# Cross attention as one pipeline over 64 units of head and batch with token-major queries; the mixer's group ends in another order, and TensorE's groups without a jump

## What is computed

```
# mixer, heads h in 8 groups of 16
hBC = silu(causal_conv(x @ Wx.T))            # hs, B, C
Y   = ((C B^T) * L_h * causal) (hs * dt) + hs * D_h   # L_h: decays of head h
g   = Y * silu(x @ Wgate.T)
out = (g * rsqrt(mean(g*g over a group)) * norm_w) @ out_proj_w.T

# cross attention, 32 query heads, 8 key heads, dimension 128
kv = concat([context, latents], axis=1)      # 128 + 128 tokens
q, k, v = rms_norm(x @ Wq) * qw, rms_norm(kv @ Wk) * kw, kv @ Wv
probs = softmax(q k^T / sqrt(128))           # 4 query heads share a key head
out = concat_heads(probs v) @ Wo
```

## Time and profile before

| | us |
|---|---|
| runs before, median of 3 | 2788.09 (2783.61 to 2791.59) |
| the profiled execution | 2793.43 |
| its span, first to last instruction | 2791.7 |
| TensorE busy in it | 2566.3 (92%) |
| VectorE, ScalarE, GpSimd busy | 1808.0, 1081.7, 1052.3 |
| mean granted TensorE clock | 0.970 |

### The profile page before, as it was taken

One profiled execution on the slowest core, in us unless ns is written; L12 is line 12 of the kernel. 1 busy time (PEld: TensorE's weight loads), 2 busy tenths in 40 slices (PEclk: granted clock), 3 DMA queues, 4 the chain that ended last, 5 costly groups with the idle time before them and its releaser, 6 DMA issues. The chain is left out here.

```text
span 2791.7 us, 40903 instructions
## 1 busy us (share of the span) xinstructions
PE 2566.3 (92%) x14344; PEld 2096.7 (75%) x14344; DVE 1808.0 (65%) x2448; ACT 1081.7 (39%) x2197; POOL 1052.3 (38%) x838
## 2 busy tenths in 40 slices
PE   7876799999999999999999999899999999999958
PEld 5444687777877778777777887788888888888846
DVE  4865696785967858769588696455463554645553
ACT  2322343333433333334334333454454444544421
POOL 3001464554655555456454565312222122222210
PEclk9988899999999999999999999999999999999989
DMA  4000331330312313213132131100100001000010
GB/s 144 1 1 16 117 118 46 110 109 32 136 53 84 114 39 120 83 66 111 44 122 98 49 110 46 31 20 23 30 17 24 19 23 30 19 23 19 12 53 31
DMA packets 61515, 163.36 MB, mean 59 GB/s; under 512 B 8336, under 2 KB 8976, under 8 KB 52944
## 3 DMA queue, kind: packets, MB, share of 16 engines
q1 hardware_dynamic: 59232, 158.14, 16.5%
q10 hardware_dynamic: 2160, 3.43, 0.4%
HBM read 158.92 MB, written 2.62 MB: 58 GB/s over the span
## 5 line engine op out<-in xcount | busy, mean ns | idle before, releaser
L196 PE MATMUL pair<-XH,d_w_hi 128*128 128x512 f32 x1160 | 479.6, 413 | 58.5 <-DVE d_gated L1394 21.2
L197 PE MATMUL pair<-XL,d_w_hi 128*128 128x512 f32 x1160 | 466.3, 402 | 0.0
L198 PE MATMUL pair<-XH,d_w_lo 128*128 128x512 f32 x1160 | 465.1, 401 | 0.0
L1371 DVE TENSOR_TENSOR_SCAN d_decay<-d_decay,m_delta 128x1024 f32<-128x1024 f32 x128 | 366.2, 2866 | 47.7 <-DMA d_decay<-token_decays 47.7
L1270 POOL TENSOR_TENSOR d_decay<-d_decay,d_cb 128x1024 f32<-128x1024 f32 x128 | 309.1, 2415 | 135.5 <-DVE d_decay L1371 125.5
L196 PEld LDWEIGHTS pair<-XH,d_w_hi 128*128 128x128 f32 x1160 | 222.6, 192 | 122.6 <-issue 41.5
L1251 POOL TENSOR_TENSOR d_w_lo<-d_w,d_w_hi 128x512 fp32r<-128x512 f32 x144 | 192.3, 1336 | 314.7 <-ACT d_w_hi L1131 314.7
L198 PEld LDWEIGHTS pair<-XH,d_w_lo 128*128 128x128 f32 x1160 | 222.6, 192 | 54.7
L197 PEld LDWEIGHTS pair<-XL,d_w_hi 128*128 128x128 f32 x1160 | 222.8, 192 | 48.0
L1356 DVE SCALAR_TENSOR_TENSOR d_hs<-pair,d_conv,d_hs 128x1016 f32<-128x1016 f32 (+2 forms) x192 | 242.9, 1265 | 20.7 <-ACT d_hs L1156 16.2
L1275 POOL TENSOR_TENSOR d_gated_lo<-d_gated,d_gated_hi 128x512 fp32r<-128x512 f32 x128 | 165.2, 1294 | 210.3 <-ACT d_gated_hi L1175 210.3
(11 more groups left out here) (275 smaller groups left out, 6083.7 us busy)
## 6 DMA issues: line engine op xcount, KB each, us to landing
d_decay<-token_decays SPq DMA_DIRECT2D x64, 1024.0 KB, 4.9
d_w<-in_L_w_groups SPq DMA_DIRECT2D x144, 256.0 KB, 2.7
e_w<-in_L_w_heads SPq DMA_DIRECT2D x80, 256.0 KB, 2.6
d_wo<-in_L_wo_groups SPq DMA_DIRECT2D x64, 256.0 KB, 4.9
X<-in_x SPq DMA_DIRECT2D x8, 256.0 KB, 10.7
b_ctx<-in_ctx SPq DMA_DIRECT2D x8, 256.0 KB, 11.8
e_ctx<-in_ctx_t SPq DMA_DIRECT2D x4, 512.0 KB, 5.1
out<-X SPq DMA_DIRECT2D x8, 256.0 KB, 2.0
```

What stands on the lines that cost most here:

```text
L196: pe.matmul(out, wh, xh, start=first, stop=False)
L197: pe.matmul(out, wh, xl, start=False, stop=False)
L198: return pe.matmul(out, wl, xh, start=False, stop=last)
L1371: v.tensor_tensor_scan(r, r, m["DELTA"][:], 0.0, ALU.mult, ALU.add).then_inc(q["decay"], 1)
```

## The change

**Attention** becomes one sequence of U = 64 units n = kh * 8 + b, written out on every engine, with no loop. Queries of a unit are projected token-major for the four query heads of the key head at once (`project_q(n)`, 12 matmuls of 512, the tokens stationary), copied by VectorE (`q_copy`), squared and summed by ScalarE in four instructions (`q_sq`), and turned by TensorE in four transposes (`turn_q`); `q_ssq` is gone. A unit's power of the sum of squares is one GpSimd instruction over four columns, 64 in all in place of 32 over eight. Keys have bank 0 alone, queries bank 1. Weights of queries and of the output have two sets of buffers, K and V one; raw weights have four slots in place of two, and are converted in the order of `ITEMS`, two per unit in the first five units of a head. X is turned in two banks at the end.

**Mixer.** TensorE's seven groups are unrolled (the other engines keep the loop). At a group's end the projection of the next group's item 0 moves ahead of the last gate, item 1 goes to the TURN pair, `out` writes banks 6 and 7, `cb` moves behind batch 0 of `out`, and the sum of squares of batch 0 into the middle of batch 1. VectorE and ScalarE follow. The load of the next group's first decays is issued at j = 7. In the last group six items of attention weights are converted, GpSimd's part between the two halves of `gated_lo`, and the context in pieces of one batch; GpSimd instead of VectorE makes its low halves.

Core of the diff:

```diff
...
+K_ITEM, V_ITEM, O_ITEM, NI = 4, 5, 6, 10
+FIRST_ITEMS, ITEMS = (4, 5, 0, 1, 2, 3, 6, 7, 8, 9), (0, 1, 2, 6, 3, 7, 8, 9, 4, 5)
+EARLY = 6
+def weights_in(n):
+    kh, b = n // NB + 1, n % NB
+    if kh == HK:
+        return ()
+    return [NI * kh + x for x in ((0, 1), (2, 3), (4, 5), (6, 7), (8, 9), (), (), ())[b]]
...
+    def w_hi(self, act, m):
+        kh, i = self.item(m)
+        act.wait_ge(self.w_in[m % 4], 16 * (m // 4 + 1))
+        if i < K_ITEM and kh > 1:
+            act.wait_ge(self.q["q_proj"], NB * (kh - 1))
+        elif K_ITEM <= i < O_ITEM and kh:
+            act.wait_ge(self.q["kv_proj"], NB * kh)
+        elif i >= O_ITEM and kh > 1:
+            act.wait_ge(self.q["out_ready"], NB * (kh - 1))
+        act.activation(self.halves(m)[0], self.WR[:, m % 4, :], ACT.Copy).then_inc(self.q["w_hi"], 1)
+    def w_lo(self, pool, m):
+        hi, lo = self.halves(m)
+        pool.wait_ge(self.q["w_hi"], m + 1)
+        pool.tensor_tensor(lo, self.WR[:, m % 4, :], hi.bitcast(F32), ALU.subtract).then_inc(self.q["w_split"], 1)
...
         def proj_pair(i):
-            return GATES if i == 1 or i in GATE_OF else IN
+            return TURN if i == 1 else GATES if i in GATE_OF else IN
+        def out_bank(b):
+            return c.bank[6 + b % 2]
...
+                def decays(g, j):
+                    if j == BC_SLOT:
+                        sp.wait_ge(q["cb_ready"], START + g + 1)
+                    else:
+                        sp.wait_ge(q["y_ready"], START + g * JT + j - RSLOT + 1)
+                    sp.dma_start(R[:, j % RSLOT, :, :].rearrange("p h t -> p (h t)"),
+                                 rows[bass.ds(g, 1), j, :].broadcast_to([P, 2 * T])
+                                 ).then_inc(rows_in[j % RSLOT], 16)
                 def group(g, last_group=False):
                     for j in range(JT):
-                        if j == BC_SLOT:
-                            sp.wait_ge(q["cb_ready"], START + g + 1)
-                        else:
...
+                        if j:
+                            decays(g, j)
+                        if j == JT - 1 and not last_group:
+                            decays(g + 1, 0)
...
                     elif i == 1:
-                        pe.wait_ge(q["gated"], START + g * JT)
+                        pe.wait_ge(q["xdt"], START + g * JT)
                     elif i in GATE_OF and GATE_OF[i] == 0:
-                        pe.wait_ge(q["tap"], START + 3 * (g * NU + units(1)[-1] + 1))
+                        pe.wait_ge(q["acc"], START + g * NB)
...
+                    pe.wait_ge(q["gated"], START + (g + 1) * JT)
+                    def ssq(b):
...
+                    for b in range(NB):
+                        pe.wait_ge(q["acc"], START + g * NB + b - 1)
+                        for j in range(JT):
+                            if j % 4 == 0:
+                                pe.wait_ge(q["g_lo"], START + 2 * (g * NB + b) + j // 4 + 1)
+                            x = (j // 4) % 2
+                            last = three_pass(pe, out_bank(b)[:, :], GH[:, x, j % 4, :], GL[:, x, j % 4, :],
+                                              WOH[:, j, :], WOL[:, j, :], j == 0, j == JT - 1)
+                            if j % 4 == 3:
+                                last.then_inc(q["out_ready"], 1)
+                            if b == 1 and j == 3:
+                                ssq(0)
+                        if b == 0 and not last_group:
+                            cb(g + 1)
+                        if b:
+                            ssq(b)
...
                         project(g, gate_item(j))
                         scan(g, j)
                     turn_hs(g, JT - 1)
+                    if not last_group:
+                        project(g + 1, 0)
                     project(g, gate_item(JT - 1))
                     scan(g, JT - 1)
                     if not last_group:
-                        project(g + 1, 0)
                         project(g + 1, 1)
                         project(g + 1, 2)
-                        cb(g + 1)
                     out(g, last_group)
...
-                with pe.Fori(0, GM - 1) as g:
+                for g in range(GM - 1):
...
-                    if not last_group:
-                        silu(g + 1, 2)
                     for b in range(1, NB):
...
+                        if last_group:
+                            if b == 1:
                                 act.wait_ge(q["gate_ready"], START + GM * JT)
-                            act.wait_ge(e.w_in[i % 2], 16 * (i // 2 + 1))
-                            act.activation(e.weight(e.WH, i), e.WR[:, i % 2, :], ACT.Copy).then_inc(e.q["w_hi"], 1)
+                            if b <= EARLY:
+                                e.w_hi(act, b - 1)
...
+                            gated_lo(g, b, (0,))
+                            if last_group and b <= EARLY:
+                                e.w_lo(pool, b - 1)
+                            elif last_group:
+                                e.ctx_lo(pool, 0)
+                            gated_lo(g, b, (1,))
...
                     if not last_group:
+                        tables(g + 1)
                         decay(g + 1, 0, 0)
-                        decay(g + 1, 0, 1)
-                        tables(g + 1)
+                        conv(g + 1, 0)
                     gated(g, JT - 1)
                     if not last_group:
-                        conv(g + 1, 0)
+                        decay(g + 1, 0, 1)
                         conv(g + 1, 1)
                         v.wait_ge(q["skip"], START + (g + 1) * JT)
                         skip_table(g + 1)
...
+                def turn_q(n):
+                    pe.wait_ge(q["q_copied"], n + 1)
                     for h in range(GQ):
-                        three_pass(pe, c.bank[2 + h // 2][:, (h % 2) * KV:(h % 2 + 1) * KV], QH[:, h, t], QL[:, h, t],
-                                   KH[:, b % 2, :], KL[:, b % 2, :], True, True).then_inc(q["scored"], 1)
...
+                for n in range(U - 3):
+                    attend(n)
+                    turn_q(n + 2)
+                    project_kv(n + 3)
+                    turn_probs(n + 1)
+                    score(n + 2)
+                    project_q(n + 3)
+                    turn_k(n + 3)
+                    out(n)
+                attend(U - 3)
+                turn_q(U - 1)
+                turn_probs(U - 2)
+                score(U - 1)
+                pe.wait_ge(q["q_lo"], U)
+                turns(0, 1)
+                out(U - 3)
+                attend(U - 2)
+                turn_probs(U - 1)
+                turns(2, 3)
+                out(U - 2)
+                attend(U - 1)
+                turns(4, 5)
+                out(U - 1)
+                turns(6, 7)
...
+                for n in range(U - 3):
+                    o_hi(n)
+                    q_hi(n + 2)
+                    evac_kv(n + 3)
+                    probs_hi(n + 1)
+                    exp(n + 2)
+                    k_hi(n + 3)
+                    q_sq(n + 3)
+                    for m in weights_in(n):
...
+                for n in range(U - 3):
+                    k_power(n + 3)
+                    for m in weights_in(n):
+                        e.w_lo(pool, m)
+                    q_power(n + 3)
+                    if n + 5 < NB:
+                        e.ctx_lo(pool, n + 5)
+                    if n >= TAIL:
+                        norm_rstd(c, pool, s, n - TAIL)
...
+                def q_copy(n):
+                    v.wait_ge(q["q_proj"], n + 1)
+                    ahead(v, "q_turned", n)
+                    ahead(v, "q_sq", n)
+                    v.tensor_copy(QN[:], QB[:, :]).then_inc(q["q_copied"], 1)
...
+                for n in range(U - 3):
+                    o_lo(n)
+                    if n > TAIL:
+                        norm_apply(c, v, s, n - TAIL - 1)
+                    q_lo(n + 2)
+                    k_var(n + 3)
+                    v_lo(n + 3)
+                    k_norm(n + 3)
+                    probs_lo(n + 1)
+                    softmax_max(n + 2)
+                    q_copy(n + 3)
+                    softmax_sum(n + 2)
+                    k_lo(n + 3)
+                    acc(n)
...
```

More of the change, by code:

```diff
@@ L1541, in _ @@
+                for m in range(EARLY, HK * NI):
+                    e.w_raw(sp, m)
             @block.tensor
             def _(pe):
[L1543 to L1555 removed]
@@ new lines, in score, with turn_probs @@
+                def score(n):
+                    pe.wait_ge(q["k_lo"], n + 1)
+                    pe.wait_ge(q["q_lo"], n + 1)
+                    ahead(pe, "exp", GQ * n)
+                    for h in range(GQ):
+                        t = slice(h * S, (h + 1) * S)
+                        three_pass(pe, score_bank(h), QH[:, n % 2, t], QL[:, n % 2, t], KH[:, n % 2, :],
+                                   KL[:, n % 2, :], True, True).then_inc(q["scored"], 1)
```

(89 more changed lines are left out.)

824 lines of the change are left out of this document (314 added, 510 removed).

## The result

| | before | after |
|---|---|---|
| median of the runs, us | 2789.84 (2783.61 to 2792.68) | 2670.68 (2669.58 to 2672.16) |
| span of the profiled execution, us | 2791.7 | 2668.7 |
| mean granted clock | 0.970 | 0.974 |

The ratio is 0.9576, with a 95% interval of 0.9558 to 0.9594: 119 us less, where 2677 us, 111 less, was forecast.

A forecast was written before the change was run, and what follows sets the result against it. TensorE's queue, busy 92%, was taken as the bound. Attention 82 us less and mixer 29 less (46 - 17) make 111 off the 2788 us median: 2677 us, with eight in ten between 2634 and 2722.

The forecast's parts named there:

- The bound: Whole kernel: TensorE, busy 92%, sets the time; a change is worth the TensorE work, idle time and half-clock matmuls it removes.
- Attention's work: Attention on TensorE: sums of squares go (52 us), four transposes per unit come (0.40); a unit costs 12.88 us, 64 cost 824.
- The K/V weights: Attention, next head's K/V weights in one buffer: TensorE waits 2.0 us seven times, 14 us, plus 8 us low clock.
- The walk: Attention: one unit timed across engines from the keys' projection's end (t = 0); k_lo ends at 9.3 against 9.9, 0.6 us slack.
- Rival (a): Waits for K/V weights and in the last group don't come, 22 and 17 us left out: 2638 us; chance 0.16.
- Start and end: Attention's first and last units: 4 us waits, 4 low clock, then 5 waits, 3 turning X, 6 behind the last output; 22 us.
- The seven group ends: Mixer: reordering takes off 27 us of waits, removed jumps 11.5 us, low clock 8 us; 46 us less.
- The last group: Last mixer group: second gated_lo queues behind weight conversion, 2.0 us for six batches; 12 us plus 5 low clock, 17 more.
- (b): Attention: the chain to k_lo, not TensorE, bounds the unit; 1.0 us per unit lost, 61 us less 14: 2724 us; chance 0.17.
- (c): GpSimd and VectorE hinder one another; two subtractions of 2.03 us lengthen seven K/V waits by 1.5 each: 2688 us; chance 0.12.
- (d): Attention's straight-line code: some 47 code packets each stop TensorE as a jump does, 170 us more: 2847 us; chance 0.05.
- The range: Forecast itself 2655 to 2700 us (query transposes -8 and +25, last group -9 and +5); eight in ten: 2634 to 2722.

The follow-up runs named there:

- run 7: The changed kernel with the four transposes of each unit's queries done twice; 2691.6 us, ratio 0.9650.
- run 10: The kernel before with each TensorE product for the queries' sums of squares done twice; 2843.1 us, ratio 1.0195.
- run 2: The changed kernel with two buffers for K/V weights, converted in a head's first unit, and one buffer each for keys, normalised keys and probabilities; 2658.3 us, ratio 0.9537.
- run 3: The changed kernel with two VectorE steps swapped at attention's end, q_lo of the last unit ahead of a norm; 2671.2 us, ratio 0.9575.
- run 4: The kernel before with only TensorE's seven mixer groups unrolled, order and attention as before; 2774.7 us, ratio 0.9951.
- run 6: The changed kernel with TensorE's mixer groups in a hardware loop again; 2687.4 us, ratio 0.9640.
- run 8: The changed kernel with an unused VectorE reduction of 1024 columns added between each unit's softmax multiply and k_lo; 2704.6 us, ratio 0.9704.
- run 1: The changed kernel with GpSimd's weight conversion in the last mixer group moved behind both gated_lo halves; 2659.5 us, ratio 0.9532.
- Run 9: The changed kernel with VectorE's add into X moved ahead of k_lo, making k_lo 0.60 us later; 2678.8 us, ratio 0.9602.
- run 5: The changed kernel with the edits of run 1, run 2 and run 3 together; 2639.9 us, ratio 0.9469.

## Right or wrong, point by point

**The bound.** Right: runs 7 and 10 move the time by nearly all that they add on TensorE.

**Attention's work.** 12.88 us per unit forecast, 12.82 measured, 4 us in all. The transposes, for which 0.40 stood with 0.10 for the matmul behind, take 0.36 start to start and 0.45 when priced (run 7). The trade of products for transposes is thus about 52 against 64 x 0.445 = 28.5 us: 24 us of the 86. Of the other 62, 34 are idle time of TensorE up to the last output matmul (58.1 us in 48 waits before, 23.7 in 16 after), 6 lie behind that matmul (12.5 against 6.1), about 8 are low clock (31.9 us of it before, 14.8 after), and about 8 follow from the price of a wait worked out below. Some 5 aren't accounted for. So the pipelining is the larger part of the change; no run did it alone, and that split rests on the prices. VectorE and ScalarE are busy 66% and 57% of a head, where 62% each was forecast.

**The K/V weights.** Place, cause and count right. The walk put GpSimd's subtraction from t = 9.3 to 11.9; measured from the boundary's own unit it runs from 9.35 to 11.84. The seven cost 14.1 us, as forecast (2.0 each); run 2 gives it back. The low clock of 8 us was too much: it fell behind two of the seven, 3.1 us. Rival (a) is out for both sets of waits.

**Start and end.** 22 us forecast. What the 64 units, the seven waits and their low clock leave of 863.6 is 26: the first units wait 6.5 us in all, not 4, and the rest is about what the nine waits of both ends cost beyond their idle time. The waits at the end are 5.0 us, as forecast, though 2.9 of them, called "issue", stand at a place that wasn't walked; run 3 shows that without it most of that time goes to the chain of the last softmax. The errors of this stage cancel in part, 868 against 863.6, and that is luck.

**The seven group ends.** -46 forecast, -54.7 measured, of which 0.5 lie ahead of the groups; the largest miss. The mixer of run 4 differs from the kernel before in the jumps alone, and from the changed kernel in the order alone. The first matmul of its last `out`, and that of the kernel before:

```profile
1674.64 0.77 PE L196 MATMUL pair<-d_wo_hi,d_gated_hi 128*128 128x512 f32 x1 [4.73 <-POOL d_gated_lo L1275]
1697.10 0.66 PE L196 MATMUL pair<-d_wo_hi,d_gated_hi 128*128 128x512 f32 x1 [4.74 <-POOL d_gated_lo L1275]
```

In the changed kernel it starts at 1642.41. Less what lies ahead of the groups, the order took off 33 us, where the prediction had 27 and one low stretch, about 29; the jumps took off 21 with the low clock that went with them, where it had 18. (By the medians the jumps are 15.7 in run 4 and 16.7 in run 6; the two profiled executions lie 3 us above and 3 below their medians.)

The main failing term is the price of a wait, which the prediction counted at its idle time. One group each at full clock, before and after, with 977 matmuls in both (columns as in the earlier trace rows):

```profile
1145.39:1325.70 180.31, 173.42 (x977) 140.70 (x977) 136.67 (x105) 67.72 (x90) 97.19 (x68) 1.00 0.24 85
980.91:1153.71 172.80, 172.35 (x977) 140.99 (x977) 135.66 (x104) 68.07 (x91) 97.09 (x67) 1.00 0.25 89
```

The group is 7.51 us shorter, but only 6.4 of that are idle time (6.88 in six waits, 0.45 in one); the other 1.07 are TensorE rows that got shorter, 0.21 us for each wait that is gone. Three other places give 0.27 to 0.30: the head boundary idles 1.75 and makes the unit 2.02 longer, run 8's wait idles 0.24 and costs 0.51, and run 6's jump idles 1.74 and, with 0.14 us less of the wait for `d_gated_lo` in the same group, makes the group 1.90 longer. The rows show where it lies. A matmul row of 512 columns in front of idle time counts with its full 0.40, though the next would have started after 0.23, and the first one behind takes longer (0.31 to the next start). The change took 33 waits out of the seven group ends, so this is about 7 us.

Three smaller terms were wrong as well. Six waits of 0.48 us ahead of the product of C and B, for ScalarE's copy, weren't counted and are gone, 2.9 us. Six low stretches went in place of five, 1.6 us. Against these, the 2.9 us of waits for `d_gated_lo` that were to go are still there, now 3.2, for batch 3 of each `out`. Together that is about 8 us, against the 7.7 missed. The price of a wait was worked out from rows and not tried by itself in the mixer.

**The last group.** +17 forecast, +19.8 measured, 18.2 taken back by run 1. The six waits of 1.62 to 1.93 us are there, for the reason given: the second `gated_lo` queued behind `w_lo`'s wait for ScalarE.

**Rivals (b), (c), (d).** The chain to `k_lo` doesn't bind a unit; its slack is 0.8 us, where 0.6 was read. Run 9 shows that 0.6 fits into the middle units, run 8 that 1.14 doesn't. Run 8 lost 34 us by it, so even that much more on this chain would have stayed short of the 47 of rival (b). (c): the two subtractions took 2.49 us together, as in the forecast, not twice 2.03. (d): the code queues carried 163 packets in place of 123, and in the middle of the stage no idle time stands without a semaphore: run 5's heads have 102.50 us busy of 102.50 through straight-line code. The jump kept its price in run 6. The Trainium skill (Runtime: NRT & Kernel Launch, section Instruction fetch mechanics) has straight-line code fetched ahead and a taken branch out of the fetched blocks stall. The runs agree on both: no idle time in run 5's heads, and 1.57 to 2.09 us at each jump of run 6.

**The range.** The bounds given for the forecast itself, -8 and -9 below it and +25 and +5 above, add up to 2660 to 2707 us, and not to 2655 to 2700. The measured time lies in both, so nothing here hangs on it. The total of 2670.7 against 2677 hides two misses of opposite sign: in the profiled execution the attention stage and the group ends gave 13 us more than forecast, and the last group took 3 more.

## To carry over

Walk a bound engine's queue start to start, and then ask of each buffer with one copy when its guard opens and who stands ahead in the two queues that refill it: that found both sets of waits, and their fixes, 12 and 11 us alone, gave 31 together. Price a wait on this kernel's matmul queue at its idle time plus about a quarter of a microsecond (0.21 to 0.30 here). The mean unit tells nothing of the first and last few, where other work is mixed in: runs 8 and 9 lost several us there that no unit in the middle showed.

## What the runs showed of the hardware

- The same idle time lowers the clock only sometimes. Seven waits of 1.75 us in each of six kernels (the changed one, runs 1, 3, 6, 8 and 9) were followed by a unit 1.55 us longer 2, 4, 2, 1, 0 and 0 times. In the changed kernel the granted clock behind the one at 2449.10 was:

```profile
2449.10:2451.70 2.60, 2.60 (x18) 2.60 (x19) 0.00 (x0) 0.00 (x0) 0.91 (x1) 0.80 0.00 0
2451.70:2454.30 2.60, 2.60 (x15) 2.60 (x15) 0.17 (x1) 0.91 (x6) 0.00 (x0) 0.54 0.00 0
```

  It drops near to one half, the lower of the two levels (1.2 against 2.4 GHz), 1.2 to 1.6 us behind the restart in the nine cases, and not at once. What decides whether it does wasn't found. It moves totals by a few us between kernels that are otherwise the same, so an edit worth under 5 us needs its own stretch read beside the total.
- A jump back in a long body costs TensorE 1.6 to 2.2 us of idle time (1.57 to 2.09 in run 6, 1.79 to 2.16 in the kernel before), with its operands ready: without the jump no wait stands at that place in either kernel.
- TensorE loses 0.21 to 0.30 us at a wait beyond the idle time that the profile shows, by the four places above.
